# Attention scores of four heads in one run of shorter matmuls, transposes in pairs of heads, and a new order of the units

## What is computed

```python
def xattn(h, ctx, mask, Wq, bq, Wk, bk, Wv, bv, Wo, bo):      # 16 heads of 32
    q, k, v = heads(h @ Wq.T + bq), heads(ctx @ Wk.T + bk), heads(ctx @ Wv.T + bv)
    scores = einsum('bhnd,bhtd->bhnt', q, k) * 32 ** -0.5 + mask[:, None]
    return merge(einsum('bhnt,bhtd->bhnd', softmax(scores), v)) @ Wo.T + bo
x = x + tanh(g_xattn) * xattn(layernorm(x), ctx, mask, ...)
x = x + tanh(g_ffn) * ffn(layernorm(x), ...)     # softmax router, best two of eight experts, three layers with gelu
```

## Time and profile before

| | us |
|---|---|
| median of 3 runs (1767.28 to 1767.84) | 1767.38 |
| the profiled execution | 1767.08 |
| its span, first to last instruction | 1765.3 |
| PE busy in it | 1747.4 |
| DVE busy | 1242.4 |
| ACT busy | 954.2 |

### The profile page before, as it was taken

How to read it: one execution, slowest core, us unless ns; L and a number is a source line. 1 busy time by engine, 2 the same in 40 slices (tenths; PEclk the granted TensorE clock), 3 DMA queues, 4 the chain that set the end, 5 groups by cost and what they waited for, 6 DMA issues and landing times.

```text
span 1765.3 us, 39880 instructions
## 1 busy us (share of the span) xinstructions
PE 1747.4 (99%) x14694; PEld 1510.8 (86%) x14694; DVE 1242.4 (70%) x3382; ACT 954.2 (54%) x1780; POOL 182.4 (10%) x271
## 2 busy tenths in 40 slices
PE   9999999999999999999999999999999999999997
PEld 8888888888888888888888877877899999999996
DVE  5577787778778777877777456666677777777773
ACT  4655656565555556565655545445555555555551
POOL 1110110111011001101100010000000111001100
PEclk9999999999999999999999999999999999999999
DMA  8982222222122222222204389998666666767661
GB/s 264 385 316 67 81 86 67 74 80 82 49 78 90 68 66 81 86 69 72 76 29 138 113 316 395 365 348 310 214 209 208 210 211 216 220 220 220 218 198 37
DMA packets 123229, 292.68 MB, mean 166 GB/s; under 512 B 17859, under 2 KB 36291, under 8 KB 123088
## 3 DMA queue, kind: packets, MB, share of 16 engines
q1 hardware_dynamic: 99664, 225.46, 37.6%
q0 software_dynamic: 23424, 65.30, 12.7%
HBM read 244.04 MB, written 46.66 MB: 165 GB/s over the span
## 4 chain that ended last, share of the span: by engine, by line
PE 94%; DVE 2%; DMA 2%; issue 1%; ACT 1%; POOL 0%; DVEq 0%; SPq 0%; POOLq 0%; ACTq 0%
PE bank_rows L2367 21%; PE bank_rows L728 16%; PE bank_rows L714 14%; PE bank_rows L776 8%; PE bank_rows L2382 6%; PE bank_rows L766 5%; PE bank_rows L787 4%; PE bank_rows L2421 4%; PE bank_rows L2448 3%; PE bank_rows L2407 3%; PE bank_rows L751 3%; PE bank_rows L803 3%; PE bank_rows L866 2%; DMA stage<-in_L_ffn_w 1%; DVE probs L1522 1%; PE bank_rows L790 1%
## 5 line engine op out<-in xcount | busy, mean ns | idle before, releaser
L1178 ACT ACTIVATE probs<-probs,neg_max 100x722 f32<-100x722 f32 x248 | 220.9, 891 | 107.7 <-DVE neg_max L1529 107.7
L1522 DVE CUSTOM_DVE_ANT_0 probs<-bank_rows,mask_sb 100x362 f32<-100x362 f32 x496 | 234.4, 529 | 8.0 <-PE bank_rows L766 7.1
L2611 DVE TENSOR_TENSOR w_low<-stage,w_high 128x1024 fp32r<-128x1024 f32 x176 | 213.0, 1223 | 35.2 <-ACT w_high L2515 34.5
L1183 ACT ACTIVATE p_t<-bank_rows 121x600 f32<-121x600 f32 x256 | 171.5, 670 | 68.7 <-PE bank_rows L776 66.6
L2515 ACT ACTIVATE w_high<-stage 128x1024 fp32r<-128x1024 f32 x176 | 183.9, 1058 | 32.9 <-DMA stage<-in_L_ffn_w 32.7
L2538 ACT ACTIVATE gelu<-bank_rows,biases 128x256 f32<-128x256 f32 x176 | 82.4, 475 | 215.9 <-PE bank_rows L2367 210.3
L2367 PE MATMUL bank_rows<-h_high,w_high 128*128 128x256 f32 x704 | 196.5, 279 | 0.0
L2367 PE MATMUL bank_rows<-h_low,w_high 128*128 128x256 f32 x704 | 196.5, 279 | 0.0
L2367 PE MATMUL bank_rows<-h_high,w_low 128*128 128x256 f32 x704 | 196.5, 279 | 0.0
L714 PE MATMUL bank_rows<-ctx_high,wk_high 128*128 128x360 f32 (+1 forms) x512 | 182.6, 357 | 0.9 <-DVE ctx_low L1488 0.8
L776 PE MATMUL bank_rows<-ident,probs 100*121 100x100 f32 x1488 | 180.6, 257 | 0.9 <-ACT p_t L1183 0.8
(11 more groups left out here) (250 smaller groups left out, 3839.4 us busy)
## 6 DMA issues: line engine op xcount, KB each, us to landing
stage<-in_L_ffn_w SPq DMA_DIRECT2D x240, 512.0 KB, 4.7
plain_w<-in_L_ffn_w SPq DMA_DIRECT2D x15, 2048.0 KB, 12.2
expert_in_rows<-filling POOLq DMA_DIRECT2D x8, 3341.0 KB, 19.7
router_rows<-in_gate_rows POOLq DMA_DIRECT2D x112, 200.0 KB, 3.3
ctx_raw<-in_ctx SPq DMA_DIRECT2D x16, 720.0 KB, 4.4
ctx_raw<-in_ctx SPq DMA_DIRECT2D x15, 724.0 KB, 4.3
xs_sb<-expert_in_rows SPq DMA_DIRECT2D x11, 514.0 KB, 5.2
b_sb<-in_L_ffn_b SPq DMA_DIRECT2D x19, 256.0 KB, 5.0
```

What stands on the lines that cost most here:

```text
L1178: nc.scalar.activation(p, p, ACT.Exp, bias=neg_max[:, h:h + 1], scale=-1.0, accum_out=exp_sum[:, h:h + 1]).then_inc(probs_ready, 1)
L1183: nc.scalar.activation(p_t[:, h % HQ, :, :].rearrange("t (k i) s -> t k (i s)", k=2), bank_rows[0:TT, 4:6, 0:3 * S], ACT.Copy).then_inc(pt ...
L1522: nc.vector.tensor_tensor_reduce(out=probs_of(b, g)[:, q, at], in0=score_bank[q][0:S, 0:size], in1=mask_sb[:, at], scale=-1.0, scalar=BIG, ...
L2611: nc.vector.tensor_tensor(lo, src, hi.bitcast(F32), ALU.subtract).then_inc(chunk_lo[which], 1)
```

## The change

- The context of 722 is cut into three pieces of 242 columns that begin at 0, 240 and 480 (two columns of each seam stand in two pieces). Banks 0 to 5 are twelve slots of 256 columns; head q of a group has the slots 3q to 3q + 2.
- `scores(b, g)` is one run a group: 36 matmuls of 242 columns. Two heads share one bank of their three, so odd heads take the pieces in another order, and in the last third of the run each odd head waits for the even head's first piece (`even_piece_done`).
- `score` on VectorE takes a head in one pass of 3 x 242 columns; `neg_max` comes out of it, and the columns that stand twice have a mask of -max in their second place. The join of the halves goes. In `scored_around` VectorE scales the output of the group before between the second and third head.
- `exps` waits for its own head's score (`scored`) and covers 726 columns.
- `transpose_probs(b, pair)` transposes two heads, twelve transposes, into the slots of these heads, whose scores have been read; it no longer waits for a copy, but `scores` of the next group waits for both copies of the group (`pt_copied`). `copy_probs` takes 1200 columns at once.
- The lists of all engines are written anew: `attend` of the group before comes right behind the run, then a unit, the first pair of transposes, a longer unit, the second pair, then the rest. Keys 31 move behind `attend` of group 0.
- The mask of a batch comes by two DMAs; banks 0 to 5 are zeroed in rows 96 to 120 at the start instead of a part of 4 and 5; the second buffer of probabilities for the last batch goes.

The lists of the first and last batch and of ScalarE change in the same manner. The core of the diff (of VectorE's `body` the new list alone):

```diff
+PIECES, PIECE, PIECE_STEP, SLOT = 3, 242, 240, 256
+TWICE = PIECE - PIECE_STEP
+TP = PIECES * PIECE
+assert PIECE_STEP * (PIECES - 1) + PIECE == T
+PIECE_ORDER = ((2, 0, 1), (1, 2, 0))
 TILES = [(0, 121), (121, 121), (242, 120), (362, 120), (482, 120), (602, 120)]
...
-EVEN_BODY = ("K31", "A3", "V3", "Y", "V4",
-             "V5", "V0", "A0", "K00", "K10",
-             "XT", "K20", "A1", "V1", "K01", "K11",
-             "K30", "CNT", "A2", "Q01", "V2", "K21")
-ODD_BODY = ("K31", "A3", "V3", "Y", "V4",
-            "V5", "V0", "A0", "Q23", "K00",
-            "XT", "K20", "A1", "V1", "K10", "K01",
-            "K30", "CNT", "A2", "V2", "K11", "K21")
...
+EVEN_BODY = ("A3", "V3", "Y", "V4", "V5",
+             "A0", "K31", "V0", "K00", "K10",
+             "A1", "K20", "V1", "XT", "K01", "K11",
+             "A2", "K30", "Q01", "CNT", "V2", "K21")
+ODD_BODY = ("A3", "V3", "Y", "V4", "V5",
+            "A0", "K31", "Q23", "V0", "K00",
+            "A1", "K20", "V1", "XT", "K10", "K01",
+            "A2", "K30", "V2", "CNT", "K11", "K21")
...
-SAME_BANK = {("CNT", "A2"), ("XT", "A2")}
...
-    score_bank, pt_bank, unit_bank = banks[0:4], banks[4:6], banks[6:8] + banks[0:2]
+    unit_bank = banks[6:8] + banks[0:2]
+    slots = bank_rows[:, 0:6, :].rearrange("p b n -> p (b n)").rearrange("p (k n) -> p k n", n=SLOT)
...
+        def load_mask(n):
+            src = batch_rows(mask, n)
+            sp.dma_start(pieces(mask_sb[:])[:, :, TWICE:],
+                         src[:, TWICE:T].rearrange("s (k t) -> s k t", k=PIECES)).then_inc(mask_loaded, 16)
+            sp.dma_start(mask_sb[:, 0:TWICE], src[:, 0:TWICE]).then_inc(mask_loaded, 16)
...
-        def scores(b, g, half):
-            after_unit(b if (g, half) == (DT - 1, 1) else b - 1, f"K{g}{half}")
-            if half == 0:
-                after_unit(*query_unit(b, g))
-            if g > 0 or half > 0 or b > 0:
-                pe.wait_ge(scored, 2 * H * b + 2 * HQ * g + HQ * half)
-            off, size = HALVES[half]
-            for step, (a, c) in enumerate(PRODUCTS):
-                for q in range(HQ):
-                    rows = slice(q * HD, (q + 1) * HD)
-                    last = nc.tensor.matmul(score_bank[q][0:S, 0:size], q_t[a][rows, g, slot(b), :],
-                                            k_hl[c][rows, g, off:off + size],
-                                            start=(step == 0), stop=(step == 2))
+        def scores(b, g):
+            for half in range(2):
+                after_unit(b if (g, half) == (DT - 1, 1) else b - 1, f"K{g}{half}")
+            after_unit(*query_unit(b, g))
+            if g > 0 or b > 0:
+                pe.wait_ge(pt_copied, PAIRS * (DT * b + g))
+            for turn in range(PIECES):
+                for step, (a, c) in enumerate(PRODUCTS):
+                    for q in range(HQ):
+                        rows = slice(q * HD, (q + 1) * HD)
+                        k = PIECE_ORDER[q % 2][turn]
+                        if (turn, step) == (PIECES - 1, 0) and q % 2 == 1:
+                            pe.wait_ge(even_piece_done, HQ // 2 * (DT * b + g) + q // 2 + 1)
+                        last = nc.tensor.matmul(slots_of(q)[0:S, k, 0:PIECE], q_t[a][rows, g, slot(b), :],
+                                                k_hl[c][rows, g, k * PIECE_STEP:k * PIECE_STEP + PIECE],
+                                                start=(step == 0), stop=(step == 2))
+                        if (turn, step) == (0, 2) and q % 2 == 0:
+                            last.then_inc(even_piece_done, 1)
             last.then_inc(scores_ready, 1)
 
-        def transpose_probs(b, h):
-            pe.wait_ge(probs_ready, H * b + h + 1)
-            if H * b + h > 0:
-                pe.wait_ge(pt_copied, H * b + h)
-            for i, (off, rows) in enumerate(TILES):
-                last = nc.tensor.transpose(pt_bank[i // 3][0:rows, i % 3 * S:(i % 3 + 1) * S],
-                                           probs_of(b, h // HQ)[:, h % HQ, off:off + rows], ident[0:S, 0:S])
+        def transpose_probs(b, pair):
+            pe.wait_ge(probs_ready, H * b + 2 * pair + 2)
+            for q in range(2 * pair % HQ, 2 * pair % HQ + 2):
+                for i, (off, rows) in enumerate(TILES):
+                    off += TWICE * (i // 2)
+                    last = nc.tensor.transpose(slots_of(q)[0:rows, i // 2, i % 2 * S:(i % 2 + 1) * S],
+                                               probs[:, q, off:off + rows], ident[0:S, 0:S])
             last.then_inc(pt_ready, 1)
 
         def attend(body, b, odd, g):
 
             bank, ready = bank_for(body, f"A{g}")
-            pe.wait_ge(pt_copied, H * b + HQ * (g + 1))
+            pe.wait_ge(pt_copied, PAIRS * (DT * b + g + 1))
...
         def body(b, odd, t, n):
 
-            scores(b, 0, 0)
-            keys(b, b, 3, 1)
+            scores(b, 0)
             attend(b, t, 1 - odd, 3)
-            scores(b, 0, 1)
             values(b, 3)
+            transpose_probs(b, 0)
             project_o(b, FRONT)
-            transpose_probs(b, 0)
+            transpose_probs(b, 1)
             project_o(b, BACK)
-            transpose_probs(b, 1)
-            values(b, 4, FRONT)
-            transpose_probs(b, 2)
-            values(b, 4, BACK)
-            transpose_probs(b, 3)
-
-            scores(b, 1, 0)
+            values(b, 4)
             values(b, 5)
-            scores(b, 1, 1)
-            values(b, 0)
+
+            scores(b, 1)
             after_unit(b, "V5")
             attend(b, b, odd, 0)
-            transpose_probs(b, 4)
+            keys(b, b, 3, 1)
+            transpose_probs(b, 2)
             if odd:
-                queries(b, "Q23", (2,))
-                transpose_probs(b, 5)
-                queries(b, "Q23", (3,))
-                transpose_probs(b, 6)
+                queries(b, "Q23", QUERY_TILES["Q23"])
+                transpose_probs(b, 3)
+                values(b, 0)
                 keys(b, n, 0, 0)
             else:
+                values(b, 0)
+                transpose_probs(b, 3)
                 keys(b, n, 0, 0)
-                transpose_probs(b, 5)
-                keys(b, n, 1, 0, FRONT)
-                transpose_probs(b, 6)
-                keys(b, n, 1, 0, BACK)
-            transpose_probs(b, 7)
-
-            scores(b, 2, 0)
+                keys(b, n, 1, 0)
+
+            scores(b, 2)
+            attend(b, b, odd, 1)
+            keys(b, n, 2, 0)
+            transpose_probs(b, 4)
+            values(b, 1)
+            transpose_probs(b, 5)
             if b + 2 < B:
                 transpose_xn(b, b + 2)
-            keys(b, n, 2, 0)
-            scores(b, 2, 1)
-            attend(b, b, odd, 1)
-            values(b, 1)
-            transpose_probs(b, 8)
             keys(b, n, *((1, 0) if odd else (0, 1)))
-            transpose_probs(b, 9)
-            m = 0 if odd else 1
-            keys(b, n, m, 1, FRONT)
-            transpose_probs(b, 10)
-            keys(b, n, m, 1, BACK)
-            transpose_probs(b, 11)
-
-            scores(b, 3, 0)
+            keys(b, n, 0 if odd else 1, 1)
+
+            scores(b, 3)
+            attend(b, b, odd, 2)
             keys(b, n, 3, 0)
-            count_pairs(b, t)
-            scores(b, 3, 1)
-            attend(b, b, odd, 2)
+            transpose_probs(b, 6)
             if odd:
                 values(b, 2)
-                transpose_probs(b, 12)
+                transpose_probs(b, 7)
+                count_pairs(b, t)
                 keys(b, n, 1, 1)
-                transpose_probs(b, 13)
             else:
                 name = "Q01" if b < B - 2 else "Q"
                 queries(b, name, QUERY_TILES[name])
-                values(b, 2, FRONT)
-                transpose_probs(b, 12)
-                values(b, 2, BACK)
-                transpose_probs(b, 13)
-            keys(b, n, 2, 1, FRONT)
-            transpose_probs(b, 14)
-            keys(b, n, 2, 1, BACK)
-            transpose_probs(b, 15)
+                transpose_probs(b, 7)
+                count_pairs(b, t)
+                values(b, 2)
+            keys(b, n, 2, 1)
 
...
         def exps(b, h):
-            if h % HQ == 0:
-                act.wait_ge(max_ready, DT * b + h // HQ + 1)
-            p = probs_of(b, h // HQ)[:, h % HQ, :]
+            act.wait_ge(scored, H * b + h + 1)
+            p = probs[:, h % HQ, :]
             nc.scalar.activation(p, p, ACT.Exp, bias=neg_max[:, h:h + 1], scale=-1.0,
                                  accum_out=exp_sum[:, h:h + 1]).then_inc(probs_ready, 1)
 
-        def copy_probs(b, h):
-            act.wait_ge(pt_ready, H * b + h + 1)
-            nc.scalar.activation(p_t[:, h % HQ, :, :].rearrange("t (k i) s -> t k (i s)", k=2),
-                                 bank_rows[0:TT, 4:6, 0:3 * S], ACT.Copy).then_inc(pt_copied, 1)
+        def copy_probs(b, pair):
+            act.wait_ge(pt_ready, H // 2 * b + pair + 1)
+            q = 2 * pair % HQ
```

(67 more changed lines are left out.)

495 lines of the change are left out of this document (196 added, 299 removed).

## The result

The changed kernel took 1777.7 us (median of 4 runs, 1776.5 to 1779.0) beside 1767.5 for the kernel before: ratio 1.0056, 95% interval 1.0044 to 1.0068. It is 10.1 us slower where I had forecast 6 us faster. Of the runs further down, one of the four of e5 took 8469 us, for which no trace gives a reason; e5's figures are those of the other three.

A forecast was written before the change was run, and what follows sets the result against it. TensorE (PE) was taken to bound the kernel: a batch lasts its list of blocks. Terms -2.0 + 0.04 + 0.5 + 0.2 + 0.9 = -0.36 us a batch, times 16, -6 us: 1761 us, range 1746 to 1778.

The forecast's parts named there:

- What bounds the kernel: Whole kernel: TensorE (PE) is full, so the change pays only by what leaves its block list, minus new waits.
- Fewer runs: Scores on PE: four runs a batch instead of eight save turns between blocks, 2.0 us a batch gained.
- shorter matmuls: Scores on PE: 36 quads of 242 columns replace 24 of 361, at 0.111 us each, +0.04 us a batch.
- rival C: Scores: the short fp32r matmuls run at plain fp32 speed, +10 us a batch, 1922 us; chance 0.06.
- The wait inside a run: Last third of a scores run: odd heads wait for the even head's first piece, 0.13 us a run, +0.5 a batch.
- Rival A: Scores and queues: the wait inside is free and the queues hold, -1.7 us a batch, 1740 to 1750; chance 0.22.
- VectorE and ScalarE beside it: Scoring passes, copies, memset and mask DMAs lie beside PE: 0.3 us a group saved on VectorE, worth nothing by itself.
- Transposes: Probabilities on PE: eight blocks of twelve transposes replace sixteen of six, +0.2 us a batch (-0.2 to +0.6).
- What comes late next: PE behind each run, mostly groups 2 and 3: late VectorE or ScalarE work makes it wait, +0.9 us a batch.
- Sum per batch: All terms of one batch together: -2.0 + 0.04 + 0.5 + 0.2 + 0.9 = -0.36 us.
- Times 16 batches (first and last are built alike): Whole kernel: the -0.36 us of one batch holds for all 16, first and last included, -6 us.
- Rival B: Between a batch's second and third run VectorE becomes the bound: +0.7 us a batch, slower, 1779 us; chance 0.22.

The follow-up runs named there:

- e5: e4 with the last batch's router matmuls moved behind the seventh pair of transposes, a whole unit of the early expert ahead of those: 1754.2 us.
- e11: e5 with batch 1's mask loaded early in one contiguous piece into free room, then copied by VectorE into the three pieces: 1744.5 us.
- e10: The changed kernel with the mask loaded by one transfer of 2888 contiguous bytes a row (scores masked wrongly, same amount of work): 1768.1 us.
- e4: The changed kernel with VectorE's choice of experts behind the fourth group's scores and, in odd batches, two router dots behind the third group's: 1756.4 us.
- e1: The kernel before with each batch's mask loaded by two transfers, meant as three 960-byte pieces and one of 8 bytes a row: 1767.9 us.

## Why the prediction was wrong, step by step

Block lengths below are from one block's first start to the next one's, means over batches 3 to 13, even and odd apart.

- *What bounds the kernel: right.* PE's list of blocks, minus the waits that the new order brings in. The waits decided.
- *Fewer runs, -2.0 us, and shorter matmuls, +0.04: right.* The scores' own blocks went from 5.4 to 4.8 us a batch, values lost 0.5 and 0.4, keys without their waits 0.6, mostly in what stands behind a run. The quads are 0.11 apart, so rival C is out.
- *The wait inside a run, +0.5: too much.* It is 0: the seventh quad follows the sixth after 0.11 us. Rival A had that half right.
- *VectorE and ScalarE beside it: right, but for the mask (below).* A head's scores follow each other at 0.83 us, the price I had, and the larger memset costs nothing: the first scores start at 34.38 us, before at 34.45.
- *Transposes, +0.2: too much, it is about -0.1.* Eight blocks of twelve take 8.7 us, sixteen of six took 8.8. The Trainium skill's 100 ns a weight load (TensorE: Matmul & The Clock Gate, LDWEIGHTS (loading the stationary operand)) would have made it +1.0; the measured 8.7 / 96 = 0.091 us a transpose decides against it here.
- *What comes late next, +0.9: mis-sized, it is 2.0.* The places were right: keys ahead of the first transposes of group 2 in odd batches (0.8 us, and 0.24 ahead of them) and of group 3 in both (0.8), the count's successor in even ones (0.43). Group 3 had been priced at 0.5, though the choice of the experts was in the table; the scores of group 3 start 0.9 to 2.1 us behind their run, where 0.27 is the least. The 0.3 us that I took off because my table also had waits for the kernel before should have stayed. In even batches the `attend` behind the run of group 0 (it belongs to the last group of the batch before) costs 0.45 us more, which nothing in the trace of before showed; it is the gap that e11 lost. (PE's idle time shows only 1.2 of the 2.0 us: a block that waits among its own matmuls counts as busy.)
- *Sum per batch, -0.36: near the measured -0.16, by two errors that cancel.* Without waits I had -1.26, it is -2.1 to -2.3; with 2.0 of waits nothing is left.
- *"Times 16 batches (first and last are built alike)": this is the step that failed.* Batch 1 is +5.8 and the last +4.7, where the sum had -0.36 for each: 11 of the 15 us that lie between the forecast and the two profiled spans. Both were in reach. Of the mask's two DMAs I wrote "a whole `attend` and three units ahead of its use: nothing", counted as if a transfer took its usual time. But the DMA share was 0.95 in batch 0 of the kernel before, and its profile has it: an issue under full queues needed a price, and the number of its packets with it. Put at nothing, this term cost 5.7 us (e10). And in the last batch the work between scores and transposes is short, and a matmul was put right behind the `attend` whose bank it takes: that one cost 1.3 us of waiting and some 1.7 of half clock, and the other waits 2.6. The second buffer of probabilities was dropped there too; whether that matters, no run shows.
- *Rival B* named the right engine and came within 2 us of the time (1779), but not by its sum: its inner batches were to lose 0.7 us each, and they gain 0.16. The time is slower because of the ends. Its place, three dots ahead of the third run's scores, was one of two; e4 moved both. Near *rival A*'s -1.7 a batch is where the inner batches stand once VectorE is on time: -1.5 in e4, -1.7 in e11, which reaches 1744.5.

What stays open: 2.6 us that e10 won beside batch 1 and the last one; 1.2 us that the changed kernel loses behind its last `attend`; the gap in the `attend` behind a batch's first run; how the waits of the last batch could go; and why the clock fell behind a wait in the last batch of the changed kernel and e4, and not behind one as long in e10.

## What to carry to other kernels

Before an order is called free for the busiest engine, take every point where it waits for a chain (scores, exponential, exponential, transposes) and ask when the first link starts: what stands ahead of it in that engine's queue is the price, and moving 2 us of routing work in every batch and 1.2 in every odd one behind the scores was worth 21 us here. Put a transfer at its worst hour, not its mean one, count its packets, and multiply by the number of batches only those that are alike: first, second and last batch get a sum of their own. An order that fits one layout of runs does harm in another, so it has to be found anew with each change of the layout. And when a run is to test the form of a transfer, look in its trace whether the packets have that form: in e1 they had not.
